# Spreading the first three row groups of each selective scan by matmul instead of by DMA, with new issue orders

## The reference, cut to what matters

```
delta = softplus(x @ Wd.T + bd)                  # (B, 512, 128)
Bmat  = x @ Wb.T + bb;  Cmat = x @ Wc.T + bc     # (B, 512, 16)
A_bar = exp(delta[..., None] * A)                # (B, 512, 128, 16)
Bx    = (delta * x)[..., None] * Bmat[:, :, None, :]
h_t   = A_bar_t * h_{t-1} + Bx_t
y_t   = sum_n h_t[:, n] * Cmat_t[n]
```

## Time and profile before

| | us |
|---|---|
| three runs | 1006.04, 493.49, 491.56 |
| median of them | 493.49 |
| the profiled execution | 490.11 |
| its span, first to last instruction | 488.3 |
| PE / DVE / ACT / POOL busy | 415.3 / 336.5 / 289.2 / 125.5 |

### The profile page before, as it was taken

How to read it: one execution, slowest core, us unless ns; L and a number is a source line. 1 busy time by engine, 2 the same in 40 slices (tenths; PEclk the granted TensorE clock), 3 DMA queues, 4 the chain that set the end, 5 groups by cost and what they waited for, 6 DMA issues and landing times.

```text
span 488.3 us, 5919 instructions
## 1 busy us (share of the span) xinstructions
PE 415.3 (85%) x2047; PEld 201.9 (41%) x2049; DVE 336.5 (69%) x616; ACT 289.2 (59%) x504; POOL 125.5 (26%) x129
## 2 busy tenths in 40 slices
PE   6979979878799999998985974538799799999995
PEld 2534533443245544443442321313566544544442
DVE  2395567687888863573779989799977634654444
ACT  5845698524146667989476896546346576821125
POOL 1100000340430009207937957745102000000000
PEclk9979999978689999999988998757989999999998
DMA  7950000744181000005009747988600000000001
GB/s 255 348 174 21 1 2 0 195 62 149 65 174 25 4 1 4 2 18 157 0 24 253 200 141 195 239 235 234 245 0 1 1 0 1 0 1 0 1 0 43
DMA packets 23613, 42.39 MB, mean 87 GB/s; under 512 B 6965, under 2 KB 12310, under 8 KB 22422
## 3 DMA queue, kind: packets, MB, share of 16 engines
q1 hardware_dynamic: 23476, 41.92, 30.0%
q10 hardware_dynamic: 108, 0.10, 0.1%
HBM read 36.93 MB, written 4.98 MB: 86 GB/s over the span
## 4 chain that ended last, share of the span: by engine, by line
PE 61%; DVE 17%; ACT 12%; issue 5%; DMA 3%; SPq 1%; POOL 1%; ACTq 0%; DVEq 0%
ACT AR L1178 8%; DVE AR L1520 7%; PE PS L900 7%; PE PS L905 6%; PE PS L927 6%; PE PS L797 4%; PE PS L814 4%; PE PS L828 4%; PE PS L701 3%; PE PS L664 3%; ACT L1174 2%; PE PS L978 2%; DMA AR<-scan 2%; PE PS L1031 2%; DVE AR L1841 2%
## 5 line engine op out<-in xcount | busy, mean ns | idle before, releaser
L1178 ACT ACTIVATE AR<-PS 128x512 f32<-128x512 f32 (+2 forms) x185 | 97.1, 564 | 109.8 <-PE PS L900 52.7
L1520 DVE TENSOR_TENSOR AR<-PS,AR 128x512 f32<-128x512 f32 (+1 forms) x120 | 79.8, 679 | 54.4 <-PE PS L905 30.4
L1178 ACT ACTIVATE AR<-AR 128x256 f32<-128x256 f32 (+3 forms) x110 | 46.7, 464 | 42.2 <-DVE AR L1520 26.2
L2158 POOL TENSOR_TENSOR AR<-AR 128x512 f32<-128x512 f32 (+2 forms) x48 | 53.7, 1126 | 54.1 <-DMA AR<-scan 27.7
L1529 DVE TENSOR_REDUCE stats<-PS 128x1 f32<-128x512 f32 (+4 forms) x88 | 44.0, 525 | 11.9 <-PE PS L800 6.2
L1174 ACT ACT_TABLE_LOAD x40 | 51.3, 1283 | 0.7
L1841 DVE TENSOR_TENSOR_SCAN AR<-PS,AR 128x512 f32<-128x512 f32 x32 | 38.8, 1213 | 1.5 <-ACT PS L1178 1.4
L797 PE MATMUL PS<-RR 97*128 97x512 bf16 (+3 forms) x128 | 33.2, 336 | 5.0 <-DVE stats L1529 4.3
L664 PE MATMUL PS<-AR,W_sq 128*128 128x256 f32 x88 | 26.0, 410 | 10.9 <-ACT AR L1178 5.9
L814 PE MATMUL PS<-RR 100*128 100x512 bf16 (+3 forms) x128 | 29.5, 302 | 2.4 <-ACT AR L1178 2.2
L1178 ACT ACTIVATE AR<-PS,W_vec 128x256 f32<-128x256 f32 (+1 forms) x46 | 24.1, 547 | 10.0 <-PE PS L664 4.7
(11 more groups left out here) (239 smaller groups left out, 726.1 us busy)
## 6 DMA issues: line engine op xcount, KB each, us to landing
AR<-scan SPq DMA_DIRECT2D x64, 256.0 KB, 3.7
RR<-in_ffn SPq DMA_DIRECT2D x1, 2688.0 KB, 11.0
RR<-in_ones SPq DMA_DIRECT2D x2, 832.0 KB
RR<-in_ones SPq DMA_DIRECT2D x2, 784.0 KB
RA<-in_moe SPq DMA_DIRECT2D x1, 1539.5 KB, 6.2
W_mla<-in_mla SPq DMA_DIRECT2D x1, 1504.0 KB, 16.0
W_late<-in_late SPq DMA_DIRECT2D x1, 1076.0 KB, 12.1
RA<-in_xa SPq DMA_DIRECT2D x1, 1056.0 KB, 8.0
```

Of the source, the lines that this page charges most:

```text
L1178: nc.scalar.activation(out_, in_, func, bias=bias, scale=scale).then_inc(*done("act", *step))
L1520: nc.vector.tensor_tensor(out_, a, b_, op).then_inc(*done("dve", *step))
L2158: nc.gpsimd.tensor_tensor(out_, a, b_, op).then_inc(*done("pool", *step))
```

## The change

A constant `FIRST = 3` divides each scan. For tiles 0 to 2:

- TensorE spreads the rows. `first_rows` is a float32 matmul of 32 rows by 128 columns by 512, with the table `chosen`, into PSUM: `dq0` to `dq2` for delta, `xq0` to `xq2` for dx. These are six new TensorE steps for each batch.
- ScalarE's exp works in place in that PSUM bank.
- VectorE makes the product `by0` to `by2` (GpSimd did).

Tiles 3 to 15 stay as they were: written to DRAM, spread by DMA and multiplied by GpSimd. There are 26 spreading DMAs for each batch where there were 32. The table `chosen` costs one small reduction on VectorE (`se`) and one small copy on GpSimd (`sd`). The order strings of all engines are replaced, from the first step of the program to the last, and `TABLES` now has 46 entries where it had 40.

```
+FIRST = 3
-            spread_rows(0, 0, NS)
+            spread_rows(0, FIRST, NS)
-            spread_rows(1, 0, 6)
+            spread_rows(1, FIRST, 6)
@@ TensorE, scan
+                def first_rows(i, rows_, to, name):
+                    g = 32 * (i % 4)
+                    mm(to, chosen[g:g + 32, :], rows_[g:g + 32, :], start=True, stop=True)\
+                        .then_inc(*done("pe", b, f"{name}{i}"))
+
+                pe.wait_ge(*after("dve", b, "dl"))
+                pe.wait_ge(*after("pool", "w", "sd"))
+                first_rows(0, A(b, 8), own(b, 1), "dq")
+                yield
+                pe.wait_ge(*after("act", b, "bB"))
+                first_rows(1, A(b, 8), own(b, 3), "dq")
+                yield
+                pe.wait_ge(*after("pool", b, "dx"))
...
+                first_rows(0, A(b, 7), own(b, 2), "xq")
+                yield
+                pe.wait_ge(*after("dve", b, "by0"))
+                first_rows(1, A(b, 7), own(b, 2), "xq")
+                yield
+                pe.wait_ge(*after("dve", b, "sc0"))
+                first_rows(2, A(b, 8), own(b, 1), "dq")
+                yield
+                pe.wait_ge(*after("dve", b, "by1"))
+                first_rows(2, A(b, 7), own(b, 2), "xq")
+                yield
@@ ScalarE, scan
+                    rows_ = own(b, 1 + 2 * (i % 2))
+                    f(rows_, rows_ if i < FIRST else scan_row(b, "dl", i), ACT.Exp, (b, f"aa{i}"), ...
@@ VectorE, scan
+                    if i < FIRST:
+                        dve.wait_ge(*after("pe", b, f"xq{i}"))
+                        dve.wait_ge(*after("act", b, "bB"))
+                        tt(scan_row(b, "dx", i), own(b, 2), A(b, 2), ALU.mult, (b, f"by{i}"))
+                        yield
@@ GpSimd, scan
-                for i in range(NS):
+                for i in range(FIRST, NS):
```

More of the change, by code:

```diff
@@ L173 @@
         *_halves("f1.ss"), "rt", *[x for k in range(U0 + 1) for x in unit_steps(k, U0, SH0, "f")],
-        *_halves("ln3.v"), "de", "bB", "bC", *[f"yn{i}" for i in range(NS // SUMMED)], "ln4.c",
+        *_halves("ln3.v"), "de", "bB", "bC", "dq0", "dq1", "xq0", "xq1", "dq2", "xq2", *[f"yn{i}" for i in range(NS // SUMMED)], "ln4.c",
         *_halves("ln4.v"), "xb.s", "xb.t", "fl0", "fl1", "fl2", "fl3", "xit",
@@ L198 @@
         *_halves("X3"),
-        "rl", "dl", *[f"{n}{i}" for i in _N for n in ("sc", "hc")], *_halves("s4"), *_halves("X4"),
+        "rl", "dl", *[x for i in _N for x in [f"by{i}"] * (i < FIRST) + [f"sc{i}", f"hc{i}"]], *_halves("s4"), *_halves("X4"),
         "xb.m", "xb.d", "lni.x", "xb.u", "xb.i", "xb.k", "xb.p", "lni.z", "xin", "ks", "kd", "bs", "bd", "xr", "xi", "yr", "yi", "ye", "yo",
@@ L203 @@
         *[x for u in _E1[2:] for x in u], *_halves("s6"), *_halves("X6")],
-    "pool": [*SPLIT, "dx", *[f"by{i}" for i in _N]],
+    "pool": [*SPLIT, "dx", *[f"by{i}" for i in _N[FIRST:]]],
 }
@@ L212 @@
             *[f"z{i}" for i in range(1, 10)], *[f"a{i}" for i in range(1, 7)],
-            *_centre("w2"), "sz", "hd.s", "hd.m",
+            *_centre("w2"), "sz", "se", "hd.s", "hd.m",
             *[f"{n}{h}" for h in HALVES for n in ("r1.", "q1.", "r2.", "q2.", "rQ0.", "qQ0.", "rQ1.", "qQ1.", "P")],
             "ed.s", "ed.m"],
-    "pool": ["kz", "va0", "va1", "e1", "fb.r", "fb.s", "fb.c", "bh", "bf", "bf1", "wz0", "wz1", "la", *[f"dc{i}" for i in range(1, 24)], "wb", "wc", "sz", "hd.c",
+    "pool": ["kz", "va0", "va1", "e1", "fb.r", "fb.s", "fb.c", "bh", "bf", "bf1", "wz0", "wz1", "la", *[f"dc{i}" for i in range(1, 24)], "wb", "wc", "sz", "hd.c", "sd",
              *[f"{n}{h}" for h in HALVES for n in ("tP", "tQ", "aP", "aQ", "U1", "U2", "V", "Q")], "ed.c"],
@@ L392, in build @@
         at = lay["hawk"][1] + lay["xa0"][1]
-        WB, WC, summed, decay, bB, bC = (RA[:, at + i:at + j] for i, j in
-                                         ((0, 128), (128, 256), (256, 312), (312, 328), (328, 329), (329, 330)))
+        WB, WC, summed, decay, bB, bC, groups = (
+            RA[:, at + i:at + j] for i, j in
+            ((0, 128), (128, 256), (256, 312), (312, 328), (328, 329), (329, 330), (330, 338)))
         def w(group, name, a=0, n=None):
@@ L625, in spread_rows @@
                     at = 32 * (i % 4) + 8 * (i // 4)
-                    for n, kind in ((0, "dl"), (1, "dx")) if i < AHEAD["dl"] else ((1, "dx"), (0, "dl")):
-                        if i == 0:
+                    for n, kind in ((0, "dl"), (1, "dx")) if i < FIRST + AHEAD["dl"] else ((1, "dx"), (0, "dl")):
+                        if i == FIRST:
                             sp.wait_ge(written[kind, b], 16)
-                        elif i >= AHEAD[kind]:
+                        if i >= AHEAD[kind] + (FIRST if kind == "dl" else 0):
                             sp.wait_ge(*(after("act", b, f"aa{i - AHEAD[kind]}") if kind == "dl" else
@@ L954, in scan @@
                 yield
+                def first_rows(i, rows_, to, name):
[10 more added lines that the diff above has]
+                pe.wait_ge(*after("pool", b, "dx"))
+                if not b:
+                    pe.wait_ge(*after("act", "w", "kp0"))
+                first_rows(0, A(b, 7), own(b, 2), "xq")
[9 more added lines that the diff above has]
+                yield
                 for k in range(NS // SUMMED):
                     pe.wait_ge(*after("dve", b, f"hc{SUMMED * k + SUMMED - 1}"))
-                    if not k and not b:
-                        pe.wait_ge(*after("act", "w", "kp0"))
                     for i in range(SUMMED * k, SUMMED * k + SUMMED):
@@ L1393, in scan @@
                 for i in range(NS):
-                    act.wait_ge(*spread_of(b, "dl", i))
-                    if i == 1:
-                        act.wait_ge(*after("act", b, "bB"))
-                    act.wait_ge(*after("dve", b, f"sc{i - 2}" if i >= 2 else "rl"))
-                    f(own(b, 1 + 2 * (i % 2)), scan_row(b, "dl", i), ACT.Exp, (b, f"aa{i}"), scale=decay[:, 4 * (i % 4) + i // 4:4 * (i % 4) + i // 4 + 1])
+                    if i < FIRST:
+                        act.wait_ge(*after("pe", b, f"dq{i}"))
+                    else:
+                        act.wait_ge(*spread_of(b, "dl", i))
+                        act.wait_ge(*after("dve", b, f"sc{i - 2}"))
+                    if not i:
+                        act.wait_ge(loads["scan"], 16 * (NS + 2))
+                    rows_ = own(b, 1 + 2 * (i % 2))
+                    f(rows_, rows_ if i < FIRST else scan_row(b, "dl", i), ACT.Exp, (b, f"aa{i}"), scale=decay[:, 4 * (i % 4) + i // 4:4 * (i % 4) + i // 4 + 1])
                     yield
@@ L1838, in scan @@
                 for i in range(NS):
+                    if i < FIRST:
+                        dve.wait_ge(*after("pe", b, f"xq{i}"))
+                        dve.wait_ge(*after("act", b, "bB"))
+                        tt(scan_row(b, "dx", i), own(b, 2), A(b, 2), ALU.mult, (b, f"by{i}"))
+                        yield
                     dve.wait_ge(*after("act", b, f"aa{i}"))
-                    dve.wait_ge(*after("pool", b, f"by{i}"))
+                    if i < FIRST:
+                        mine(b, f"by{i}")
+                    else:
+                        dve.wait_ge(*after("pool", b, f"by{i}"))
                     nc.vector.tensor_tensor_scan(A(b, 14 + i % 2), own(b, 1 + 2 * (i % 2)), scan_row(b, "dx", i), 0.0,
@@ L2120, in shared_program @@
                 yield
+                red(groups, w("sq", "id").rearrange("p (g e) -> p e g", e=32)[:, 0:8, :], ALU.add, ("w", "se"))
+                yield
                 dve.wait_ge(loads["moe0"], 16)
@@ L2328, in shared_program @@
                 centre("moe0", 34, U0, "hd")
+                yield
+                pool.wait_ge(*after("dve", "w", "se"))
+                for b in range(B):
+                    pool.wait_ge(*after("pe", b, "xa.s1"))
+                ts(chosen.rearrange("p (n e) -> p n e", e=8), groups.unsqueeze(1).to_broadcast([128, NS, 8]), 1.0, None,
+                   ALU.mult, ALU.bypass, ("w", "sd"))
                 yield
```

5 lines of the change are left out of this document (3 added, 2 removed), and 50 rows, old and new, of tables (TABLES, TURNS).

## The result

The changed kernel took 505.75 us (median of four runs, 501.82 to 509.3), the kernel before 492.52. Medians here are over all runs of a kernel, while ratios leave out those that lay far above the rest: 1006.04 of the kernel before, and later 507.94 (128 rows, batch 1 alone) and 505.97 (the mended kernel). The ratio is 1.0288, with an interval of 1.023 to 1.0347: slower by more than the 2% that can be told from no change. 492.4 had been forecast, 485.5 to 499.5 as the range.

The account below looks back on a forecast made before the run. VectorE was taken as near its own sum of work in the scans, with PE never idle from 400 us. Stage +0.9, collision -1.1 and table loads +0.9 made +0.7 on a mean of 491.7: 492.4 us, range 485.5 to 499.5.

Parts of the forecast that it names:

- `a.sc0` 4.0 us earlier: Batch 0's first scan starts at 258.8 instead of 262.83, as the DMA trip goes and ScalarE's exp is next late.
- other moves before 250 I put at 0 +-3: Order moves before 250 us: no net effect, 0 +-3 us, as PE and VectorE keep the same work per stage.
- The price of a row matmul, 0.86 or up to 1.92: Each 32-row by 128-column matmul on TensorE: 0.86 us taken, 1.92 us as the upper bound.
- From sc0 to sc3, 8.5 us: Batch 0's first three scans and VectorE work among them take 8.5 us, so sc3 starts 2.3 us earlier, at 267.3.
- rival D: TensorE held in its order: batch 1's experts slip by the 3.4 us of fg1, 495.8 us; chance 0.05.
- Four pieces behind sc3, 4.9 us: Table pieces moved from the DMA gap and ahead of X3 to between sc3 and sc7 cost VectorE 4.9 us.
- Batch 1's trip: Delta to batch 1's first scan: 8.8 us leave the path, but the scan starts only 1.4 us earlier.
- Batch 1's scan, +3.3 -1.4: Extra VectorE work behind batch 1's sc0 adds 3.3 us and vanishing idle time takes 1.4; last hc15 ends +0.5.
- The collision of `ed.c`, -1.1: Moving GpSimd's 3.60 us operation away from batch 1's two spectral products, which took 4.28 instead of 1.4, gains 1.1 us.
- Table loads, +0.9: Six further ScalarE table loads, 7.7 us in all, cost 0.9 us at ScalarE's 12% of the chain.
- rival C: ScalarE becomes last among batch 0's scan and its 7.7 us of table loads are paid: 500.3 us; chance 0.15.
- Rival B: VectorE closes its idle gaps (-3.3) and the removed collision pays fully (-2.9), loads hidden: 485.5 us; chance 0.20.

Follow-up runs that it names:

- 128 rows, batch 1 alone: Kernel before in its old orders and loads, only batch 1's first three rows by TensorE and VectorE, with matmuls over all 128 rows: 499.6 us, ratio 1.0139.
- the mended kernel: Changed kernel with 128-row matmuls, the old order up to batch 0's X3, and fg1 ahead of xq1: 494.72 us, ratio 1.0087.
- The wide form: Changed kernel with row matmuls over all 128 rows (tables zero outside their 32 rows) in place of 32: 496.91 us, ratio 1.0111.
- a double dose: Changed kernel with six of ScalarE's table loads between 200 and 300 us issued twice: 505.29 us, ratio 1.0285.
- each half of this change alone: Kernel before with only the new orders and table loads: 503.77 us; changed kernel's row matmuls with the old orders and 40 loads: 512.58 us.
- the experts in the gap: Changed kernel with batch 1's expert matmuls fg1 and fu1 ahead of xq1, in TensorE's wait for by0: 502.43 us, ratio 1.0211.

## Why the prediction was wrong, by its own steps

- **`a.sc0` 4.0 us earlier: 1.2.** From `dl` it was 7.1 us, 6.3 forecast. Of the 2.8 us, 2.0 are the late `dl`: "other moves before 250 I put at 0 +-3" was +2.0 in the trace, 1 to 3 in the runs. The other 0.8 is a wrong sign: `sc0` didn't wait for ScalarE, whose `aa0` ended at 260.8, but for VectorE's own queue, which came from batch 1's routing to `by0` only at 260.75, 1.4 us behind the end of `xq0`.
- **The price of a row matmul, 0.86 or up to 1.92.** The three ahead of `by0` took 1.98 us and not 2.58, for a reason that the sum didn't have (see the last section). One alone took 1.12 at full clock, and 2.07 at half clock, above the upper bound.
- **From sc0 to sc3, 8.5 us: 13.4. Here it failed.** The 8.5 is VectorE's own work, with no wait in it, and of TensorE's order only `fg1` was priced ("so I take nothing, up to 3.4"). But `by2` needs `xq2`, which stands behind `xq1`, `fg1`, `dq2`, `fu1` and `fwt`; at half clock it ended at 271.3, and VectorE waited 5.05 us for it. `sc3` came 5.4 us late and not 2.3 early. This is the largest error of the sum: 7.7 us, of which 2.8 are the later `sc0` and 4.9 this stretch. `hu1` came at 273.2 instead of 265, not for want of `fg1` or `fu1` (ended at 264.7 and 268.7) but behind `by2` and `sc2`. By mechanism it was rival D (0.05), TensorE held in its order. I had weighed that order for batch 1's experts alone, and at the full clock's prices.
- **Clock.** No term of the sum had one. The rows at half clock were there, 0.66 from 262 to 266.5 of the kernel before among them, and 1.92 stood as a price only. The wide form, which takes away the low clock at this place, gave 8.8 us.
- **Four pieces behind sc3, 4.9 us: 5.7,** and `a.s3` to `b.s0` 43.1 for 38.9, where 39.2 had been forecast. By the runs their price is some 4.5 while the clock is low, 2.8 with the wide form, 0 in the mended kernel. The forecast let 4.1 us of idle time go; part came back as waits for the later experts (1.32 us for `fu2` at 277.5).
- **Batch 1's trip:** from `b.dl` to `b.sc0` 6.2 us for 9.5, as forecast in kind; and VectorE's work filled it, `a.s11` to `b.s0` 12.9 for 13.0. That nothing is won there was right.
- **Batch 1's scan, +3.3 -1.4:** 37.4 for 36.9 in the trace, 38.7 to 38.9 with the wide form (+1.9, the sum's own), 41 to 42 in most traces with 32 rows.
- **The collision of `ed.c`, -1.1:** gone. The two products take 1.29 us; but `b.s15` to the end is 1.6 us longer all the same, so no gain came through.
- **Table loads, +0.9 (rival C up to 7.7):** nothing that shows, with a double dose. C is out. The row is 1.30 us from a load's start (258.84) to the next exp (260.14), as before. The 2.66 us a switch that the Trainium skill gives (ScalarE: Activation LUTs, "What ACT_TABLE_LOAD costs") doesn't show here either.
- **Rival B** (idle time goes): VectorE's idle time from 250 to 350 rose from 9.6 to 11.9 us, and `b.sc0` came 9.6 us late.

With the clock held, the forecast's number would have stood: 496.9 and 494.7 lie within the range, 4.5 and 2.3 above 492.4. Its steps would not: even in the wide kernel `sc3` started at 271.05 and not at 267.3.

What stays open: why the wide form brought nothing in batch 1 alone (no trace is read there), how the clock's fall and its long stay share the 8.8 us, and the last 3 to 4 us of the mended kernel, of which the trace puts 1.0 on `b.s0` (coming later), 1.8 on batch 1's scan and 1.4 behind it.

## What to carry to other kernels

When TensorE takes over a copy or a broadcast, its price isn't its own duration: ask what stands ahead of it in TensorE's order, which engine waits for it, whether it makes TensorE wait, and how many rows it uses; then cost it and the matmuls behind it at half clock as well. A DMA trip that the order has filled with other work is worth little, because that work has to go somewhere; and in batch 1, where 1.36 us of idle time were there to win, the waits for the row matmuls cost more than that. And an order made for one data flow can't be judged with another: each half of this change alone cost about as much as the whole or more.

## What the runs showed of the hardware

- Behind waits of 2.1 to 2.4 us beside row matmuls the granted clock fell to the 1.2 GHz level with 32 rows (five kernels), behind 1.70 with 64 and behind 2.22 with 128. With 32 and 64 rows in the mix it then stayed at 0.50 to 0.52 for 13 us in which TensorE was busy nearly all the time; with 128 rows, in the one trace where it fell, it was back at 1.00 from 266 on.
- The Trainium skill (TensorE: Matmul & The Clock Gate, "The HAM clock gate") makes the clock depend on how busy TensorE has been. The falls agree with that. But in the changed kernel 13.00 busy us of 13 left it at 0.51, while the kernel before got it back soon behind 2.35 of 4 us busy, and busy time alone doesn't explain that. What differs is the form of the matmuls.
- Two 32-row matmuls on different groups of rows ran at the same time: in the changed kernel `dq0` (rows 0 to 31) and `dq1` (rows 32 to 63) began 6 ns apart (257.392 and 257.398), so three row matmuls took 1.98 us. Three with 64 rows, of which two share their rows, took 2.84, three with 128 rows 2.74. One 32-row matmul by itself was no cheaper than one with 128 rows, 1.12 for 1.13 behind a wait at full clock (the row of the run with the experts in the gap):

```profile
262.15 1.12 PE L942 MATMUL PS<-AR,M 32*128 32x512 f32 x2
```

- VectorE's 128x256 pair took 2.46 us beside a GpSimd product and 0.88 without; six more table loads of 1.28 us cost nothing that shows.
- Code that is the same from 318 us on ran batch 1's scan in 37.4 us at a granted clock of 1.00 from 318 to 330, and in 41.0 at 0.60: one profile of a stretch whose clock differs between executions is no measurement of it.
